# Mixing stage rewritten: four chunks in flight, straight code, division in attention's tail, gate products moved out of the memory stage

## The reference

```
x = x + attention(ln(x))        # 16 heads of 16, softmax, x residual, w_out
x = x + ffn(ln(x))              # ternary weights
x = x + memory(ln(x))           # see below
x = x + ffn(ln(x))

memory(hidden):
  k, v, q = causal_dwconv(hidden @ W{k,v,q}.T)            # 4 taps, 64 wide
  alpha = mean(sigmoid(hidden @ aW.T + ab) * 0.1)
  eta   = mean(sigmoid(hidden @ eW.T + eb) * 0.9 + 0.05)
  theta = mean(softplus(hidden @ tW.T + tb) * 0.1)
  for each chunk of 128 tokens:                           # states S, W = (W1, W2)
    g = 0.1 * grad of |silu(k W1') W2' - v|^2, clipped to norm 1
    S = eta S - theta g;  W = (1 - alpha) W + S           # per token, as a scan
    out = silu(q W1_t') W2_t'
  out = retrieved @ Wo.T;  out = out * rsqrt(mean(out^2) + eps) * norm_g
  return out * (hidden @ gW.T + gb)
```

## Time and profile before

| what | us |
|---|---|
| median of 3 runs | 1433.18 (1421.13 to 1443.31) |
| the profiled execution, its span | 1433.8, 1432.0 |
| PE busy | 1209.4 (84%) |
| DVE busy | 1014.0 (71%) |
| ACT busy | 772.0 (54%) |
| POOL busy | 218.8 (15%) |
| mean granted TensorE clock | 0.889 of full |

### The profile page before, as it was taken

How to read it: one execution, slowest core, us unless ns; L and a number is a source line. 1 busy time by engine, 2 the same in 40 slices (tenths; PEclk the granted TensorE clock), 3 DMA queues, 4 the chain that set the end, 5 groups by cost and what they waited for, 6 DMA issues and landing times. The chain is left out here.

```text
span 1432.0 us, 21407 instructions
## 1 busy us (share of the span) xinstructions
PE 1209.4 (84%) x6402; PEld 626.6 (44%) x6402; DVE 1014.0 (71%) x1650; ACT 772.0 (54%) x1553; POOL 218.8 (15%) x286
## 2 busy tenths in 40 slices
PE   6996999999999999999999984666775628998995
PEld 3652333333333333333333323444554327787774
DVE  6649889889888898887988702467777443575463
ACT  4541777777767777777777740144343332322221
POOL 5206000000000000000000001122322113434331
PEclk9995999999999999999999956788788657999797
DMA  8962133321333213333030002233332343353330
GB/s 280 205 265 35 20 60 54 61 38 34 61 54 61 42 31 56 61 53 55 24 56 16 16 15 75 102 114 111 110 121 96 107 124 95 107 156 92 92 103 30
DMA packets 106046, 117.70 MB, mean 82 GB/s; under 512 B 22381, under 2 KB 73901, under 8 KB 105965
## 3 DMA queue, kind: packets, MB, share of 16 engines
q1 hardware_dynamic: 97080, 103.71, 30.6%
q10 hardware_dynamic: 8896, 13.22, 2.6%
HBM read 63.48 MB, written 52.26 MB: 81 GB/s over the span
## 5 line engine op out<-in xcount | busy, mean ns | idle before, releaser
L563 DVE TENSOR_REDUCE maxes<-ps_m 128x2 f32<-128x1024 f32 x512 | 598.8, 1218 | 79.0 <-PE ps_m L601 77.8
L542 ACT ACTIVATE prob<-ps_s 128x512 f32<-128x512 f32 x1024 | 532.7, 602 | 182.3 <-PE ps_s L612 175.7
L612 PE MATMUL ps_s<-q_stack,k_stack 50*128 50x512 f32 x1024 | 330.2, 486 | 13.5 <-ACT prob L542 13.5
L622 PE MATMUL ps_o<-prob,v_ones 128*32 128x512 f32 x2048 | 285.0, 630 | 0.0
L612 PEld LDWEIGHTS ps_s<-q_stack,k_stack 50*128 50x128 f32 x1024 | 142.8, 190 | 324.3 <-ACT prob L542 295.1
L601 PE MATMUL ps_m<-k_stack,q_stack 48*128 48x512 f32 x1024 | 206.1, 460 | 27.4 <-DVE maxes L563 24.8
L601 PEld LDWEIGHTS ps_m<-k_stack,q_stack 48*128 48x128 f32 x1024 | 100.9, 193 | 106.5 <-DVE maxes L563 101.8
L510 POOL COPY v_ones<-v_all 128x512 f32 (+1 forms) x16 | 9.9, 616 | 580.7 <-PE ps_o L622 580.7
L1097 PE MATMUL p_a<-w_out,p_o 128*128 128x256 f32 x128 | 44.2, 520 | 41.9 <-POOL p_o L817 21.3
L1097 PE MATMUL p_a<-ternary,p_zT 128*128 128x256 f32 x128 | 49.1, 567 | 28.0 <-ACT p_zT L874 28.0
L622 PEld LDWEIGHTS ps_o<-prob,v_ones 128*32 128x32 f32 x2048 | 40.9, 109 | 68.0 <-ACT prob L542 51.5
(11 more groups left out here) (194 smaller groups left out, 1437.4 us busy)
## 6 DMA issues: line engine op xcount, KB each, us to landing
qk_parts<-p_parts SPq DMA_DIRECT2D x32, 512.0 KB, 5.3
q_stack<-qk_parts SPq DMA_DIRECT2D x96, 128.0 KB, 4.6
k_stack<-qk_parts SPq DMA_DIRECT2D x96, 128.0 KB, 7.8
oT<-o_sb SPq DMA_DIRECT2D x32, 256.0 KB, 2.1
x_all<-in_x_dram SPq DMA_DIRECT2D x8, 512.0 KB, 10.6
p_o<-oT SPq DMA_DIRECT2D x16, 256.0 KB
p_inverse_sums<-inverse_sums SPq DMA_DIRECT2D x16, 256.0 KB
x<-p_x SPq DMA_DIRECT2D x8, 512.0 KB, 4.0
```

The source lines that it names most:

```text
L542: act.activation(prob[at % P_RING][:, h], ps_s[:, (GH * at + h) % S_RING], ACT.Exp, scale=HD ** -0.5).then_inc(exp_done, 1)
L563: dve.tensor_reduce(maxes[:, i // 2, i % 2], ps_m[:, i % M_PAIRS], AX.X, ALU.max).then_inc(m_taken, 1)
L612: pe.matmul(ps_s[:, (GH * (UNITS * slot + KT * qc + kt) + h) % S_RING], r32(k_st[slot][rows, pair, kt * P:(kt + 1) * P]), r32(q_st[slot][r ...
L622: ins = pe.matmul(ps_o[32 * h:32 * h + 32], v_st[slot][:, kt, h], prob[(UNITS * slot + KT * qc + kt) % P_RING][:, h], start=kt == 0, stop= ...
```

## The change

- The head outputs and inverse sums get buffers outside of the stages (`heads`). In the last attention group SP loads those of chunks 0 and 1, and POOL divides them (`load_heads`, `divide_heads`). POOL there also multiplies the gate's weights and bias with norm_g.
- `mix` has no loops any more. Iteration `it` (from -3 to 7) works on chunk it+3 (product with w_out), it+2 (both layernorms, ternary product), it+1 (projections, sigmoids, gate product) and it (taps, scans, keys).
- The softplus subtraction on POOL is replaced by a second, accumulating matmul with -1/64.
- The gate products are made in `mix` (`gate_products`), copied by ACT, stored, and loaded by `remember`, where POOL adds the bias; `remember` loses its gate products and `take_gate`.
- The late sums are waited for by DVE ahead of the first addition instead of later. All stores of terms are issued by SP. eta, keep and some others have two buffers. The row of ones for the stacks comes from a tile that exists already.

```
@@ load_heads / divide_heads, new, used by attend and mix
+def load_heads(sp, oT, inverse, heads, n):
+    b, half = divmod(n, T // CHUNK)
+    at = slice(half * CHUNK, (half + 1) * CHUNK)
+    for c in range(CH):
...
+        sp.dma_start(heads["o"][n % 2][:, c], src).then_inc(heads["loaded"][n % 2], 16)
...
+        sp.dma_start(heads["inverse"][n % 2][:, c], sums.unsqueeze(1).to_broadcast([H // CH, HD, CHUNK])).then_inc(heads["loaded"][n % 2], 16)
+
+def divide_heads(pool, heads, n):
+    pool.wait_ge(heads["loaded"][n % 2], 16 * 2 * CH * (n // 2 + 1))
+    o = heads["o"][n % 2]
+    pool.tensor_tensor(o[:], o[:], heads["inverse"][n % 2][:], ALU.mult).then_inc(heads["divided"], 1)
@@ attend, sync
                     sp.dma_start(inverses_of(inverse, early, per_head), sums[:]).then_inc(inverse_out, 16)
+                    sp.wait_ge(inverse_out, 16)
+                    load_heads(sp, oT, inverse, heads, 0)
+                    load_heads(sp, oT, inverse, heads, 1)
                 store(g, 0)
@@ attend, gpsimd
             place_v(NG - 1, 0)
...
+            pool.tensor_tensor(const["w_gate"][:], const["w_gate"][:], norm_g.to_broadcast([P, CH, C]), ALU.mult).then_inc(bias_added, 1)
+            pool.tensor_tensor(rows[:, ROW_GB:ROW_GB + 1], rows[:, ROW_GB:ROW_GB + 1], norm_g, ALU.mult).then_inc(bias_added, 1)
+            divide_heads(pool, heads, 0)
+            divide_heads(pool, heads, 1)
@@ mix, gpsimd
-                pool.tensor_tensor(soft[HI], relu_t[HI], sig_t[HI], ALU.subtract).then_inc(soft_ready, 1)
...
+            for it in ITERATIONS:
+                if valid(it + 2):
+                    deviation(it + 2, 0, var_z, rstd_z)
+                if it + 4 > 1 and valid(it + 4):
+                    if valid(it):
+                        pool.wait_ge(conv, 2 * it + 2)
+                    divide_heads(pool, heads, it + 4)
+                if valid(it + 2):
+                    deviation(it + 2, 1, var_h, rstd_h)
+                if valid(it):
+                    if valid(it + 2):
+                        pool.wait_ge(h_ready, it + 3)
+                    memory_terms(it)
@@ mix, scalar
+            for it in ITERATIONS:
+                if valid(it + 1):
+                    project_copies(it + 1)
+                if valid(it + 2):
+                    copy_zT(it + 2)
+                if valid(it + 1):
+                    oldest_taps(it + 1)
+                    log_sigmoid(it + 1)
+                    means(it + 1)
+                if valid(it):
+                    keys_values(it)
+                if valid(it + 1):
+                    take_gates(it + 1)
+                    theta(it + 1)
+                if valid(it + 2):
+                    copy_hT(it + 2)
@@ mix, vector
+            for it in ITERATIONS:
+                if it == -2:
+                    dve.wait_ge(sums_moved, 16)
+                    dve.reciprocal(late_sums[:], late_sums[:]).then_inc(inverted, 1)
+                if valid(it + 2):
+                    add_out(it + 2)
+                if valid(it):
+                    tap(it, 1)
+                if valid(it + 2):
+                    put_z(it + 2)
+                if valid(it):
+                    tap(it, 2)
+                    tap(it, 3)
+                    scan_decays(it)
+                if valid(it + 2):
+                    add_ffn(it + 2)
+                if valid(it):
+                    scan_keeps(it)
+                if valid(it + 2):
+                    put_h(it + 2)
+                if valid(it):
+                    products_of_keys(it)
@@ mix, tensor
-                    ins = pe.matmul(ps_p[:, 1, i:i + 1], soft[HI, i * P:(i + 1) * P], const["mean"][HI, 0:1], start=True, stop=True)
+                    pe.matmul(ps_p[:, 1, i:i + 1], relu_t[HI, c], const["mean"][HI, 0:1], start=True, stop=False)
+                    ins = pe.matmul(ps_p[:, 1, i:i + 1], sig_t[HI, c], const["minus_mean"][HI], start=False, stop=True)
@@ remember
-                        ins = pe.matmul(ps_g[:, b // 2, cols(b % 2, C)], hT[s][:, g, b], w_gate[:, g], start=g == 0, stop=g == CH - 1)
...
-                pool.tensor_tensor(gated[:], gate[:], rows[:, ROW_NORMG:ROW_NORMG + 1].to_broadcast([P, B, C]), ALU.mult).then_inc(gated_ready, 1)
+                pool.tensor_tensor(gate[s][:], gate[s][:], rows[:, ROW_GB:ROW_GB + 1].to_broadcast([P, B, C]), ALU.add).then_inc(gated_ready, 1)
...
-                dve.tensor_tensor(gate[:], ps_g.rearrange("p a (k n) -> p (a k) n", n=C), rows[:, ROW_GB:ROW_GB + 1].to_broadcast([P, B, C]),
```

681 lines of the change are left out of this document (312 added, 369 removed).

## The result

The median of the changed kernel is 1381.84 us (1373.26 to 1382.76, 4 runs); the kernel before, on the same chip, took 1431.55 us. The ratio is 0.966 (0.959 to 0.973). The profiled execution took 1373.26 us, span 1371.0, at a mean granted clock of 0.915. The forecast was 1374 us, with a range of 1345 to 1402.

The account below looks back on a forecast made before the run. Mixing was taken to wait on chains running from engine to engine, with no engine full. Mixing -63.6, its tail +0.5, memory stage -1.8 and clock +5 sum to -59.9, so 1433.8 becomes 1374 us, range 1345 to 1402.

Parts of the forecast that it names:

- Division in the attention tail, -11.4: End of attention: dividing heads of chunks 0 and 1 there starts mixing's first product at 860.1 instead of 871.55 us.
- Late sums, +2: Start of mixing: DVE waits for the late sums before its first addition, 0 to 5 us, taken as +2.
- Fill: Mixing before the first projection: projection 0 starts at 892.6 instead of 925.60 us, one w_out product taken as 3.7.
- A full iteration, 25.2 + 1.55: Mixing: one iteration's chain takes 25.2 us, plus 1.55 for the division beside the scans, giving 26.7.
- I take the tap as the nearest row: +1.55: Mixing: POOL's division holds a DVE scan as it held a tap, +2.0 on DVE, costing 1.55 us per iteration.
- a rival: Mixing: iterations near 31 us because PE's slack is only 0.6 and products run at 1.2 GHz; about 1408 us, chance 0.12.
- 23.5, five times 26.7 and 24.0: Mixing: predicted lengths of the seven intervals between projections 0 and 7, against seven of 30.2 us before.
- Tail, +0.5: Mixing behind projection 7: the last G starts 25.4 us after it, against 24.95 before, so +0.5.
- Memory stage, -1.8 and +5: Memory stage: earlier state products in the first step with outputs save 1.8 us; one more long step costs 5.
- the clock term: Memory stage: PE's clock takes back 5 us through one more long step, bounds -15 and +15.
- PE's holes grow, so more steps are long: Memory stage: longer PE waits lead to 1.2 GHz products and 31 us steps; one more long step, +5 us.
- One sign of being wrong: Memory stage: the prediction is wrong if it shows 1.2 GHz outside of turn to ternary product.

Follow-up runs that it names:

- e5: Changed kernel with loads and divisions of heads of chunks 0 and 1 moved back from attention's tail to the start of mixing: 1388.38 us, ratio 0.972.
- e6: Changed kernel with 16 unread matmuls put back in the memory stage where the gate products stood: 1378.09 us, ratio 0.965.
- e7: Changed kernel with 6 unread matmuls of 128x256 ahead of the turn of hid in mixing: 1372.78 us, ratio 0.964.
- e4: Changed kernel with POOL's addition of the gate's bias in the memory stage waiting until z (first step with outputs: gradients) is done: 1360.10 us, ratio 0.945.
- e8: Changed kernel with POOL's division in mixing moved one iteration later, to its start, beside DVE's first additions: 1356.42 us, ratio 0.949.
- e10: Changed kernel with the edits of e8 and e4, and theta means ahead of the gate products in mixing: 1345.58 us, ratio 0.936.

## Why the prediction was right, and where it was not

The kind of change and the time came out right; the four stages did not all, and part of the closeness is luck: the profiled execution entered mixing 7.3 us before the forecast's 860.1, for no reason in the change, and from the first product to the end it took 6.2 us more than the sum (518.2 against 512.0). The runs at 1378 to 1382 are the fairer comparison with 1374: some 6 us too low.

**Division in the attention tail, -11.4: right.** The first product starts 0.0 us behind mixing's first issue, before 11.6; undone in e5, 12.0. That the work costs attention nothing is not shown by one trace; the twelve traces that have it reach mixing's first issue at 859.1 us on average (848.8 to 867.2), the two without it at 860.0 and 862.9.

**Late sums, +2: too much.** Alone, that load let DVE start 2.4 us after its issue (852.74 to 855.10), where 9.2 had been the bound. DVE waited another 0.17 us for PE after that.

**Fill: right in the sum, by luck.** 32.3 against 32.5. Inside it the product with w_out took 5.78 instead of the 3.7 that I took, and the 2 us of the late sums, which did not come, gave that back.

**A full iteration, 25.2 + 1.55: the base was right, the price left out the clock.** The only iteration with scans and no division ahead of the last took 25.1, the last 22.8 against 22.55 (25.2 - 3.7 + 1.05). With a division they took 28.9 on average: 3.8 instead of 1.55. The step that fell short is "I take the tap as the nearest row: +1.55". The hold itself was right, 2.0 us at one scan per chunk, and where it lies, and so was its price as long as the clock stays up: 26.8 and 26.7 us in one iteration each of e5 and e6. But I let it end with DVE. It made hid late, so that PE stood 1.4 us behind matmuls of one column, and in all four iterations turn and product fell in part to 1.2 GHz (+0.9 and +0.6 to +1.9). I had even measured PE's slack there as 0.6 us and used it only for a rival. And the sum charged the division in six intervals where four have it. Against 23.5, five times 26.7 and 24.0 the intervals came out 1.1 longer in the first, 8.9 in the four with a division together, and 1.6 and 1.2 shorter in the last two: the 7.1 between 181.0 and 188.1, rounded.

**Tail, +0.5: too little.** It grew by 3.0. I let chunk 6 wait for ACT until +14.4 behind projection 7, from a projection at full clock, though the earlier trace rows shows the last one with 8.01 us. It took 8.01 again, and DVE's key norms started at +16.4; their own 1.4 us I left out. So the last G starts at +28.8 instead of +25.4, and what follows it was 0.9 us shorter than before:

```profile
1073.17 8.01 PE L1146 MATMUL p_p<-p_hT,w_p 128*128 128x512 f32 x12 [1.11 <-ACT p_hT L953]
...
1089.53 0.22 DVE L1058 CUSTOM_DVE_ANT_0 p_squares<-p_kT 128x64 f32<-128x64 f32 x1 [2.58 <-ACT p_kT L936]
...
1102.00 0.68 DVE L1053 TENSOR_TENSOR p_G<-p_p,p_C 128x512 f32<-128x512 f32 x1
```

In e7, where that projection took 5.42, the stretch was 39.5.

**Memory stage, -1.8 and +5: both wrong, sum near.** For the second step I expected gradients 1.8 us sooner. They came 3.7 us later counted from z1, 2.1 of it because POOL's bias no longer waits for DVE's gate and fell onto the factor, most of the rest because output products ran at 1.2 GHz. The state products, which before had started 1.0 us behind the gradients, started 2.8 us later and took 2.9 us more. The step went from 19.2 to 25.0. The sign of the clock term was wrong, too: instead of one long step more there were two fewer, 1 in place of 3. The reasoning "PE's holes grow, so more steps are long" failed because the hole moved ahead of products that are hidden; the wait ahead of the turn, said to grow to about 3 us, shrank to 0.3 to 1.4 in the steps that were short. One sign of being wrong came true: PE ran at 1.2 GHz outside of turn to ternary, in the state products of every step (before, only of the first) and in output products of the second. By the starts of z1, the second step gives +5.8, the two steps that are no longer long -4.0 and -4.9, the other four +0.9 together, and the stretch behind the last z1 +2.2: the 0 that was measured. The Trainium skill, TensorE: Matmul & The Clock Gate, Part 1, has the throttled clock as the default that activity releases. The granted clock of this stage did fall, from 0.86 to 0.81, as that says; the time did not rise.

That POOL's operation stretches z to 3.40 stood in the prediction as a fact that stays. Moving that operation is the largest gain that a run found in this stage (e4).

## What to carry to other kernels

Before you cost a POOL instruction at nothing, look at which DVE rows run beside it, and list them by how many inputs lie in SBUF: 2.36 us on POOL held a scan, a tap, a norm, z or a factor of 0.15 us by about two microseconds, and nothing beside additions from PSUM and statistics. A buffer that is filled earlier lets such an instruction start earlier, and so changes what it collides with. When matmuls are taken out of an engine that waits, ask where its wait lies afterwards and whether the products behind it are on the path.

## What was unexpected of the hardware

- The held time follows the POOL instruction and not the size of the DVE one: a DVE instruction of 128x4 was held from 0.15 to 2.29 us as a scan of 128x128 was from 0.42 to 2.42, and z, which has only one tensor and scalars per partition, from 1.38 to 3.40. So an instruction need not read two full tensors to be held.
- The same stretch of PE's work ran at either clock level. Behind 8 matmuls of one column and a wait of 1.43 us, turn and product with w_out took 1.97 and 5.50 us in the changed kernel and 1.09 and 3.62 in one iteration of e5; behind the same matmuls and a wait of 0.33 or 0.34 the product took 5.30 and 3.62 in two iterations of e8. What decides is open.
- Full matmuls that nobody reads can be worth their time: with 5 of them (2.4 us) the memory stage took 3.3 us less than in e10, with 10 (4.6 to 4.8 us) 2.8 more. Each is one profile, of a stage that read 2.2 us apart in e4 and e10 with one code.
- In the profile one float32 matmul of 128x256 is two rows, whose starts lie 0.23 us apart at 2.4 GHz.
